# Both parts' sums in one run, the layers in one block a step, later loads, and a subtraction moved to GpSimd

## The reference: what is computed

```python
h = jnp.maximum(_layernorm(x, axis=-1), 0.0)                       # x: 12500 x 128
agg = segment_sum(edge_attr_48, dst, num_segments=12500)           # 412500 x 48, dst is sorted
u = graph_globals[0]                                               # 64 numbers, the same for all
z = relu(concatenate([h, agg, u], axis=1) @ W1 + b1)               # W1: 240 x 256
out = x + z @ W2 + b2                                              # W2: 256 x 128
```

## Time and profile before

| | us |
|---|---|
| median of 3 runs (lowest, highest) | 277.83 (276.93, 278.12) |
| the profiled execution | 278.3 |
| its span, first to last instruction | 276.5 |
| busy in the span: PE, PE's weight loads, DVE, ACT, POOL | 243.8, 195.0, 239.1, 147.3, 75.5 |
| moved by DMA | 94.53 MB, mean 342 GB/s |

### The profile page before, as it was taken

The page is one execution under the profiler, slowest core; times in us unless marked ns, Lnnn a source line. Parts: engine busy times, 40 slices in busy tenths (PEclk is TensorE's granted clock), DMA queues, the critical chain, the costliest instruction groups (busy, mean ns, idle before and its releaser), DMA issues.

```text
span 276.5 us, 17261 instructions
## 1 busy us (share of the span) xinstructions
PE 243.8 (88%) x7448; PEld 195.0 (71%) x7448; DVE 239.1 (86%) x579; ACT 147.3 (53%) x315; POOL 75.5 (27%) x89
## 2 busy tenths in 40 slices
PE   7445688998999999999999999999999988998893
PEld 5344676786697688778777877886787776777572
DVE  2993589999899999999999899899899899886394
ACT  3466285465365556555555655564465454557640
POOL 8470310412213303303312311321330330234210
PEclk9977599999999999999999999999999999999998
DMA  7999999999999999999999999999999999981101
GB/s 247 377 383 260 367 382 381 381 381 382 389 384 387 392 388 385 388 391 385 388 392 387 386 390 391 383 387 382 372 390 390 385 384 369 382 295 59 40 38 57
DMA packets 70876, 94.53 MB, mean 342 GB/s; under 512 B 4324, under 2 KB 64260, under 8 KB 70854
## 3 DMA queue, kind: packets, MB, share of 16 engines
q1 hardware_dynamic: 69802, 94.29, 95.3%
q10 hardware_dynamic: 956, 0.00, 0.2%
q0 software_dynamic: 96, 0.00, 0.0%
HBM read 87.88 MB, written 6.40 MB: 341 GB/s over the span
## 4 chain that ended last, share of the span: by engine, by line
DMA 63%; PE 14%; DVE 9%; issue 7%; SPq 3%; POOL 1%; ACT 1%; DVEq 0%; POOLq 0%
DMA out<-out_buf 56%; PE group_bank L1021 5%; DMA edge_buf<-in_edge_attr 3%; DMA x_buf<-in_x 3%; PE out_bank L1087 3%; SPq L326 2%; DVE onehot L776 2%; PE window_bank L1044 2%; DVE rel_rows L731 2%; PE hidden_bank L1004 1%; POOL out_buf L513 1%; PE hidden_bank L1069 1%; DVE tile_sums L839 1%; DVE bn L818 1%; PE out_bank L1059 1%
## 5 line engine op out<-in xcount | busy, mean ns | idle before, releaser
L776 DVE TENSOR_TENSOR onehot<-rel,const_bank 128x896 f32<-128x896 f32 (+1 forms) x122 | 122.8, 1026 | 7.4 <-PE group_bank L1021 7.2
L1021 PEld LDWEIGHTS group_bank<-edge_buf,onehot 128*32 128x32 f32 x6454 | 78.8, 112 | 21.3 <-issue 15.9
L1021 PE MATMUL group_bank<-edge_buf,onehot 128*32 128x48 f32 x6454 | 86.1, 210 | 8.8 <-issue 6.1
L513 POOL TENSOR_TENSOR out_buf<-mlp_out,xb_buf 128x512 f32<-128x512 f32 x23 | 29.5, 1283 | 163.5 <-DMA out<-out_buf 137.3
L1069 PE MATMUL hidden_bank<-normed_t,w_node 128*128 128x512 f32 (+1 forms) x100 | 50.5, 586 | 0.1
L1087 PE MATMUL out_bank<-w_sb,hidden 128*128 128x128 f32 x384 | 47.7, 277 | 1.4 <-ACT normed_t L587 1.4
L1087 PEld LDWEIGHTS out_bank<-w_sb,hidden 128*128 128x128 f32 x384 | 44.7, 192 | 1.6 <-issue 1.6
L576 ACT ACTIVATE normed_x<-x_buf,shift,inverse 128x128 f32<-128x128 f32 x98 | 40.4, 482 | 5.9 <-DVE shift L833 5.9
L1073 PE MATMUL hidden_bank<-tile_sums,w_high 112*128 112x512 f32 (+1 forms) x50 | 38.7, 775 | 0.0
L501 POOL TENSOR_TENSOR xb_buf<-x_buf,b_rows 128x512 f32<-128x512 f32 (+1 forms) x25 | 31.9, 1277 | 22.8 <-DMA x_buf<-in_x 10.5
L608 ACT ACTIVATE hidden<-hidden_bank,hidden_bias 128x512 f32<-128x512 f32 (+1 forms) x50 | 31.8, 668 | 4.7 <-PE hidden_bank L1075 4.6
(11 more groups left out here) (92 smaller groups left out, 217.0 us busy)
## 6 DMA issues: line engine op xcount, KB each, us to landing
edge_buf<-in_edge_attr SPq DMA_DIRECT2D x97, 672.0 KB, 10.4
edge_buf<-in_edge_attr SPq DMA_DIRECT2D x24, 504.0 KB, 10.2
...
```

The lines of the kernel that those rows point to most:

```text
L513: pool.tensor_tensor(out_buf[k.parity][:, 0:nj, :], mlp_out[:, 0:nj, :], xb_buf[k.third][:, 0:nj, :], ALU.add).then_inc(out_added, 1)
L776: dve.tensor_tensor(onehot[:, c0:c0 + cols, :], rel[:, r0:r0 + cols].unsqueeze(2).to_broadcast([P, cols, WINDOW]), ramp_const.unsqueeze(1) ...
L1021: done = pe.matmul(group_bank[h][WINDOW * j:WINDOW * (j + 1), n * F_EDGE:(n + 1) * F_EDGE], onehot[:, (g0 + j) * EDGES_PER_ROW + r, :], ed ...
```

## The change

1. **PE.** Both parts of a step are summed in one run. Then comes one block, `layers_and_places(s)`: `turn_x(s-1)`, `first_layer(s-2)`, both `place` of step s itself (before: part 1 was placed a step later), `second_layer(s-2)`. It stands in the program three times, under `If`.
2. **DVE.** In a step: the five one-hots of the next step with the two `low_sums` of this one between them, `invert`, both `add_window`, both `make_placing` of the next step, `moments` and `join_moments` of the next tile (before: of this one).
3. **GpSimd** makes the low part of the tile sums (`tile_low`) for tiles 0 to 21, ahead of `add_out`; DVE keeps the last three.
4. **ACT**'s order follows; `tile_high` goes to the end of a step.
5. **SP.** Blocks 1 to 3 of `dst` are loaded in steps 0, 1 and 2, and turned in steps 3, 5 and 7. The loads of weights are split: four biases and global rows after step 1's edges, four weight blocks inside step 0.
6. **End.** The last tile is transposed into `group_bank[1]` instead of the bank that `second_layer` needs.

```diff
@@ -362,34 +364,37 @@
                 for row in (0, STACK_LOW):
                     sp.dma_start(w1_edge[row:row + F_EDGE, :], w1[F_NODE:F_NODE + F_EDGE, :])\
                         .then_inc(weights_in, 16)
-                sp.dma_start(w1_global[:, :], w1[F_NODE + F_EDGE:, :]).then_inc(weights_in, 16)
-                sp.dma_start(global_col[:, :], graph_globals[0:1, :].rearrange("a g -> g a")).then_inc(weights_in, 16)
-                sp.dma_start(b1_col[:, :], b1.rearrange("(c p) -> p c", p=P)).then_inc(weights_in, 16)
                 sp.dma_start(w1_node[:, :], w1[0:F_NODE, :]).then_inc(weights_in, 16)
                 sp.dma_start(w2_sb[:, :, :], w2.rearrange("(c p) n -> p c n", p=P)).then_inc(weights_in, 16)
+
+            def load_bias():
                 sp.dma_start(b2_rows[:, :], bass.AP(tensor=b2.tensor, offset=0, ap=[[0, P], [1, F_NODE]]))\
-                    .then_inc(weights_in, 16)
+                    .then_inc(b2_in, 16)
+                sp.dma_start(w1_global[:, :], w1[F_NODE + F_EDGE:, :]).then_inc(bias_in, 16)
+                sp.dma_start(global_col[:, :], graph_globals[0:1, :].rearrange("a g -> g a")).then_inc(bias_in, 16)
+                sp.dma_start(b1_col[:, :], b1.rearrange("(c p) -> p c", p=P)).then_inc(bias_in, 16)
 
             load_dst(0)
             load_part(At(0), 0)
             load_part(At(0), 1)
-            load_dst(1)
             load_x(At(0))
             load_part(At(1), 0)
-            load_dst(2)
-            load_dst(3)
-            load_weights()
             load_part(At(1), 1)
+            load_bias()
             load_x(At(1))
             for s in range(steps):
                 if s >= 1 and s + 1 < tiles:
                     load_x(last_tile() if s + 1 == tiles - 1 else At(s + 1))
                 if s + 2 < steps:
                     load_part(At(s + 2), 0)
+                if s == 0:
+                    load_weights()
                 if s >= 4:
                     store(At(s - 4))
                 if s + 2 < steps:
                     load_part(At(s + 2), 1)
+                if 1 <= s + 1 < blocks:
+                    load_dst(s + 1)
             for k in range(steps - 4, tiles - 2):
                 store(At(k))
             sp.wait_ge(last_added, 1)
...
@@ -513,7 +518,16 @@
                 pool.tensor_tensor(out_buf[k.parity][:, 0:nj, :], mlp_out[:, 0:nj, :], xb_buf[k.third][:, 0:nj, :],
                                    ALU.add).then_inc(out_added, 1)
 
+            def tile_low(k):
+                pool.wait_ge(tile_high_ready, k.value + 1)
+                pool.tensor_tensor(sums_tile(k, STACK_LOW), agg_tile(k), sums_tile(k, 0).bitcast(fp32), ALU.subtract)\
+                    .then_inc(tile_low_ready, 1)
+
             for s in range(steps):
+                if 2 <= s < full_steps:
+                    pool.wait_ge(xb_ready, s)
+                    tile_low(At(s - 2))
+                    pool.wait_ge(tile_low_ready, s + 1)
                 if s >= 3:
                     add_out(At(s - 3))
...
@@ -652,46 +665,46 @@
             act.sem_inc(turned_copied, 1)
             zero_strip(2)
             copy_sums(At(0), 0)
-            relative(1)
             zero_strip(3)
             copy_sums(At(0), 1)
-            copy_rel(1)
-            relative(2)
             deviate(At(0))
             normalise(At(0))
-            load_ends(1)
+            deviate(At(1))
             copy_sums(At(1), 0)
-            copy_rel(2)
-            relative(3)
+            copy_sums(At(1), 1)
             copy_turned(At(0))
-            split_weights()
-            copy_rel(3)
-            deviate(At(1))
             bias()
-            copy_sums(At(1), 1)
             normalise(At(1))
+            tile_high(At(0))
             for s in range(2, full_steps):
-                tile_high(At(s - 2))
                 if s >= 3:
                     copy_out(At(s - 3))
+                if s % 2 == 0 and 2 <= s // 2 <= blocks:
+                    copy_rel(s // 2 - 1)
                 copy_sums(At(s), 0)
+                if s == 2:
+                    split_weights()
+                copy_sums(At(s), 1)
                 copy_turned(At(s - 1))
                 deviate(At(s))
                 relu_hidden(At(s - 2))
-                copy_sums(At(s), 1)
                 normalise(At(s))
-            second, last = At(tiles - 2), last_tile()
-            tile_high(At(tiles - 3))
+                tile_high(At(s - 1))
+                if s % 2 == 0 and s // 2 < blocks:
+                    relative(s // 2)
+                if s == 2 * blocks + 2:
+                    load_ends(1)
+            third, second, last = At(tiles - 3), At(tiles - 2), last_tile()
             copy_out(At(tiles - 4))
+            copy_turned(second)
             deviate(last)
-            copy_turned(second)
+            normalise(last)
             copy_sums(At(steps - 1), 0)
-            normalise(last)
-            relu_hidden(At(tiles - 3))
+            relu_hidden(third)
+            copy_turned(last, group_bank[1])
             tile_high(second)
-            copy_turned(last)
             tile_high(last)
-            copy_out(At(tiles - 3))
+            copy_out(third)
...
                 n = At(s + 1)
-                add_window(At(s - 1), 0)
-                low_sums(At(s - 1), 1)
-                if n.value * GROUPS % P + GROUPS > P:
-                    dve.wait_ge(rel_ready, 2 * (n.value * GROUPS // P + 2))
-                make_onehot(n, 0)
                 if s >= 2:
-                    tile_low(At(s - 2))
-                moments(At(s))
-                make_onehot(n, 1)
-                join_moments(At(s))
-                make_placing(At(s), 0)
-                make_onehot(n, 2)
-                add_window(At(s - 1), 1)
-                low_sums(At(s), 0)
-                if s == 1:
-                    dve.wait_ge(w1_high_ready, 1)
-                    dve.tensor_tensor(w1_low[:, :], w1_edge[:, :], w1_high[:, :].bitcast(fp32), ALU.subtract)\
-                       .then_inc(w1_split, 1)
+                    if n.value * GROUPS % P + GROUPS > P:
+                        dve.wait_ge(rel_ready, 2 * (n.value * GROUPS // P + 2))
+                    make_onehot(n, 0)
+                    if s == 2:
+                        dve.wait_ge(w1_high_ready, 1)
+                        dve.tensor_tensor(w1_low[:, :], w1_edge[:, :], w1_high[:, :].bitcast(fp32), ALU.subtract)\
+                           .then_inc(w1_split, 1)
+                    make_onehot(n, 1)
+                    low_sums(At(s), 0)
+                    make_onehot(n, 2)
+                    low_sums(At(s), 1)
+                    make_onehot(n, 3)
+                    make_onehot(n, 4)
                 invert(At(s))
-                make_onehot(n, 3)
-                make_onehot(n, 4)
-                make_placing(At(s), 1)
-                if s == blocks:
+                add_window(At(s), 0)
+                add_window(At(s), 1)
+                make_placing(n, 0)
+                if s + 1 < full_steps:
+                    make_placing(n, 1)
+                k = last_tile() if s + 1 == tiles - 1 else n
+                moments(k)
+                join_moments(k)
+                if s == 2 * blocks + 2:
                     dve.wait_ge(rel_ready, 2 * blocks)
                     c0 = first_last * EDGES_PER_ROW
                     link(dve.memset(rel[0:masked_rows, c0:c0 + EDGES_PER_ROW], -1.0))
                     link(dve.memset(rel[0:masked_rows + 1, c0:c0 + masked_rest], -1.0))
             second, last = At(tiles - 2), last_tile()
-            add_window(At(full_steps - 1), 0)
-            low_sums(At(full_steps - 1), 1)
-            moments(last)
-            make_placing(At(steps - 1), 0)
+            invert(last)
...
             def turn_rel(b):
-                rows = min(P, n_groups - b * P)
                 pe.wait_ge(rel_rows_ready, b + 1)
+                if not isinstance(b, int):
+                    pe.wait_ge(hidden_copied, b * 4 + 6)
                 for h, (r0, r1) in enumerate(halves):
-                    if b >= 1:
-                        pe.wait_ge(rel_ready, 2 * b)
                     for r in range(r0, r1):
                         done = pe.transpose(
-                            hidden_bank[h][:, (r - r0) * P:(r - r0) * P + rows],
-                            rel_rows[0:rows, b % 2, :].rearrange("g (p r) -> g r p", r=EDGES_PER_ROW)[:, r, :],
-                            ident[0:rows, 0:rows])
+                            hidden_bank[h][:, (r - r0) * P:(r - r0 + 1) * P],
+                            rel_rows[:, :].rearrange("g (p r) -> g r p", r=EDGES_PER_ROW)[:, r, :], ident[:, :])
                     done.then_inc(rel_turned, 1)
...
             turn_rel(0)
             keep_clock(8, window_bank[0])
+            def layers_and_places(s):
+                turn_x(s.plus(-1))
+                first_layer(s.plus(-2))
+                place(s, 0)
+                place(s, 1)
```

(51 more changed lines are left out.)

73 lines of the change are left out of this document (43 added, 30 removed).

## The result

The changed kernel takes 280.48 us (median of 4 runs, 280.23 to 280.86), the kernel before 277.70 in the same job (4 runs, 276.93 to 278.12). The ratio is 1.0105, 95% interval 1.0079 to 1.0130: slower by 1.1%. Forecast were 277.7 and no change.

A forecast was written before the change was run, and what follows sets the result against it. Transfers through a full queue were taken as the bound. Small loads -0.42 and PE's order +0.35 gave -0.1 us: 278.2 against the profiled 278.3, or 277.7 against the median 277.83; range 275.3 to 279.3.

The forecast's parts named there:

- rival C: PE's longer loop program stops it about 3 us at step 9; absorbed in mid-run, 280.7 if in the tail; chance 0.05.
- Compute at the start does not take the queue's cover: At the start, some 3.4 MB or 9 us are in flight when SP comes to wait for tile 0's `normalise`.
- the room in a step: In steady steps, PE has some 0.45 us to spare and DVE 0.8 to 1.4 us.
- the transfers' hold on the steps: In steady steps, 3.79 MB at 388 GB/s take 9.8 us, which is the step; a lighter DVE buys nothing.
- the turning of `dst`: `dst` blocks 1 to 3, turned in steps 3, 5 and 7, at least two steps ahead of need: hidden.
- The transfers' price of the small loads: At the start, the dip loses 2.15 us, mostly engines busy with slow, small transfers; moving the loads gains only 0.4 us.
- rival A: The dip at the start was queue starvation, so 2.15 us go: 275.7; chance 0.30 with lesser forms.
- My sentence on transfers under 64 KB: Small loads: transfers under 64 KB are dominated by their descriptors wherever they stand, so the whole 2.15 us would stay.
- The low part on GpSimd: In each step, DVE loses 0.69 us and GpSimd finishes with 1.5 us slack: nil, other end -0.5 us.
- rival B: The low part comes too late from GpSimd, costing 0.1 us in each of 20 steps: 279.7; chance 0.12.
- the tail behind step 24's start: After the last steps' sums, PE's list is the same and DVE's chain decides: nil, ends -0.4 and +0.5 us.
- VectorE's waits for x: Sign of being right: DVE's waits for x grow as its busy share falls by some 7 points; no size given.

The follow-up runs named there:

- e6: Changed kernel without the third copy of `layers_and_places`, both `step_base` loads ahead of `invert`, step 0's places directly behind their turns; 277.79 us, ratio 1.0008.
- e17: Changed kernel with the first turn's part of the second guarded block placed ahead of the layers' copies, same instruction order; 283.25 us, ratio 1.0197.
- e12: e6 with `normalise` of step 1 out from behind `bias`, and `invert` of step 1 and `turn_x` of step 0 earlier; 278.12 us, ratio 1.0013.
- e8: Kernel before with only the low part of the tile sums moved to GpSimd; 277.81 us, ratio 1.0011.
- e13: Changed kernel with the low part of the tile sums back on VectorE, behind the step's second one-hot; 293.79 us, ratio 1.0584.
- e2: Changed kernel with both `step_base` register loads of VectorE moved ahead of `invert`; 279.07 us, ratio 1.0052.
- e14: Kernel before with the eight small loads issued behind step 1's second part and x of tile 1; 277.69 us, ratio 1.0006.
- e1: Changed kernel with the third copy of `layers_and_places` removed; 278.9 us, ratio 1.0046.

## Why the prediction was wrong

**The step that failed first** is rival C's dismissal: "PE already stands still for about 3 us three times in its first turn. One such stop in mid-run is absorbed by the full queue". I looked for a stop at step 9 and gave nothing for the first turn itself. There the changed kernel has two more stops (4.55 and 2.87 us; all five are 5.5 us longer than the three were), and it moved the places of step 0 behind the fourth. The row was in the prediction, and the diff moved that very code. It costs 4.2 us at the start of step 3: e6 takes 3.4 of them back, and e17, which starts step 3 another 3.3 us late, is 2.8 us slower than the changed kernel. C's own number, 280.7, is near the 280.48 by luck: after 45 us PE shows no stop for its program of even 0.3 us.

**The second** is "Compute at the start does not take the queue's cover". I counted bytes in flight up to one wait of SyncE, at tile 0; the next, for `normalise` of step 1, was reached at 38.4 us and ended at 44.6, and the seventh to ninth slices are low. This cost little: the last edges land 0.4 us later, and e12, without the wait, is not faster.

**The third** is the room in a step: "0.45 us to spare" for PE and "0.8 to 1.4" for VectorE. They were idle times before, in another order. I had read the transfers' hold on the steps from two waits for x at 238 and 248 us; there is no such wait before 188 us, so for most of the run the engines set the pace of the steps (e8 made them faster there), and nothing absorbs an early stop. In the new order PE's room was right in size (9.3 us against 9.8), but the turning of `dst`, which I called hidden, takes it away in steps 3, 5 and 7. VectorE had 0.2 us: it holds steps 11 to 18 at 9.59 us, although it is busy for 17 us less over the run. e13 adds 0.69 us and gets nearly all of it in time, e2 takes away two exposed register loads and gets 0.3 a step.

**What held.** The transfers' price of the small loads (e14), where rival A is refuted: the changed kernel's dip shrank to 4.5 x (1 - 337/385) = 0.56 us, but 0.6 + 0.3 us turn up at 56 to 60 us, with waits mixed in. My sentence on transfers under 64 KB reaches less far than I used it, though: only four of the eight loads are smaller than that (48, 48, 1 and 0.2 KB). The low part on GpSimd, nil: it waits only for ScalarE, PE's products with `tile_sums` wait 0.0 us for it, and e8 finds no cost, so rival B is refuted. The landing time near 10 us (9.5), the busy share of VectorE (6 points down), and the tail behind step 24's start (20.4 us in both; the 0.6 us from step 23 on, outside my end of -0.4, were won in that step). One sign of being right failed: VectorE's waits for x did not grow, they fell from 2.3 to 1.2 us:

```profile
L831 DVE BATCH_NORM_STATS2 bn<-x_buf 128x6 f32<-128x128 f32 x98 | 21.1, 272 | 1.2 <-DMA x_buf<-in_x 1.2
```

**Open.** Three shares of the late start and the missing room were not tried alone. The turning of `dst` in steps 3, 5 and 7 is read from the timeline only. PE's granted clock was 0.50 from 30 to 43 us, against 0.66 (30 to 38) and 1.00 (38 to 43) before, so a product of `place` took 0.31 us for 0.23. And e1's median is 1 us lower than its profile explains. What brings the stop in `sum_bias` and what moved it to the loop's jump in e17 is open too. The stops end 6.0 to 6.9 us apart (15.65, 22.04, 28.04, 34.97, 41.39), as the 16 KB packets do, and roughly as in the kernel before; but neither length nor order of the code foretold which packet PE would wait for. Whether an emptier queue brings them faster was not tried.
